# One-hot records stored with the two halves of different gathers, and a target loop of six gathers on a ring of six

## The reference, cut to what matters

```python
ef = concatenate([nf[src], nf[dst], traj[:, None]], axis=-1)
msg = leaky_relu(ef @ We.T + be, negative_slope=0.01)
red = segment_sum(msg, dst, num_segments=nf.shape[0])
h = leaky_relu(concatenate([nf, red], axis=-1) @ Wn.T + bn, negative_slope=0.01)
```

## Time and profile before

| | us |
|---|---|
| median of 3 runs | 10442.16 |
| lowest and highest | 10429.43, 10443.02 |
| profiled execution, first to last instruction (span) | 10466.8 |
| span less the median of the runs | 24.6 |
| first target phase, gathers L1695, first to last start | 3310.8 to 4534.3 |
| layers' target phases together, gathers L1832, first to last start | 5273.9 to 10353.2 |

### The profile page before, as it was taken

How to read it: one execution, slowest core, us unless ns; L and a number is a source line. 1 busy time by engine, 2 the same in 40 slices (tenths; PEclk the granted TensorE clock), 3 DMA queues, 4 the chain that set the end, 5 groups by cost and what they waited for, 6 DMA issues and landing times. The chain is left out here.

```text
span 10466.8 us, 546251 instructions
## 1 busy us (share of the span) xinstructions
PE 8877.0 (85%) x200294; PEld 7617.9 (73%) x200294; DVE 8717.3 (83%) x16671; ACT 7435.1 (71%) x19555; POOL 4345.7 (42%) x4286
## 2 busy tenths in 40 slices
PE   7999999546997666659988888999888989989987
PEld 6999999324775555558877777787777768877775
DVE  6999999456998999978878787787887878778877
ACT  7888887003666999966777777677777767677776
POOL 0000000455002777734455555345555534455553
PEclk9999999656999999969999999999999999999998
DMA  1000000023666888849988888698788859978875
GB/s 44 8 10 8 8 8 6 19 42 101 210 209 203 253 253 254 248 115 290 294 256 248 248 249 215 208 293 273 248 248 248 243 160 293 295 247 249 249 247 150
DMA packets 1298246, 1948.78 MB, mean 186 GB/s; under 512 B 192607, under 2 KB 831081, under 8 KB 1297257
## 3 DMA queue, kind: packets, MB, share of 16 engines
q1 hardware_dynamic: 1052054, 1285.20, 36.7%
q0 software_dynamic: 245248, 650.66, 24.2%
q10 hardware_dynamic: 304, 4.93, 0.1%
HBM read 1225.54 MB, written 719.25 MB: 186 GB/s over the span
## 5 line engine op out<-in xcount | busy, mean ns | idle before, releaser
L1832 POOL DMA_INDIRECT work<-rows,oct_at x1752 | 2148.6, 1226 | 1609.9 <-DVE work L1957 1448.1
L1663 PEld LDWEIGHTS bank<-work 128*128 128x128 fp8e4 (+1 forms) x56064 | 1938.1, 98 | 477.3 <-issue 289.5
L1663 PE MATMUL bank<-work 128*128 128x64 bf16 x56064 | 2107.4, 193 | 110.8 <-issue 87.7
L1957 DVE TENSOR_TENSOR work<-bank,work 128x512 f32<-128x512 f32 x1752 | 1206.8, 689 | 768.1 <-PE bank L1908 616.1
L1908 PE MATMUL bank<-work 128*128 128x64 bf16 x42048 | 1600.5, 193 | 186.8 <-issue 138.5
L1607 PE MATMUL bank<-work 128*128 128x64 bf16 x34560 | 1567.4, 193 | 5.7 <-issue 5.7
L1908 PEld LDWEIGHTS bank<-work 128*128 128x128 fp8e4 x42048 | 1391.5, 98 | 214.4 <-issue 171.8
L1607 PEld LDWEIGHTS bank<-work 128*128 128x128 fp8e4 x34560 | 1412.4, 98 | 174.5 <-issue 9.7
L1858 ACT CAST work<-bank 128x512 bf16<-128x512 f32 x1752 | 1026.4, 586 | 542.6 <-issue 374.2
L1626 DVE TENSOR_SCALAR work<-bank,part 128x512 fp8e4<-128x512 f32 x1440 | 1029.0, 750 | 283.0 <-PE bank L1587 282.6
L1961 DVE SCALAR_TENSOR_TENSOR bank<-work 128x512 f32<-128x512 f32 x1752 | 1216.9, 695 | 4.5
(11 more groups left out here) (363 smaller groups left out, 20361.0 us busy)
## 6 DMA issues: line engine op xcount, KB each, us to landing
work<-hits_g SPq DMA_DIRECT2D x1752, 256.0 KB
rows<-work SPq DMA_DIRECT2D x1440, 256.0 KB
hits_g<-work SPq DMA_DIRECT2D x584, 256.0 KB
rows<-work SPq DMA_DIRECT2D x480, 260.0 KB
work<-hits_s SPq DMA_DIRECT2D x720, 128.0 KB, 3.1
work<-rows,oct_at POOLq DMA_INDIRECT x2336
hits_s<-work SPq DMA_DIRECT2D x240, 128.0 KB
side<-meta POOLq DMA_DIRECT2D x720, 20.0 KB, 3.1
```

Source lines behind the costliest of these rows:

```text
L1663: last = ten.matmul(to[:, 0:D], hits_of(j), piece_of(j), start=j == 0 and k == 0, stop=j == OCT - 1 and k == 2, skip_group_check=True)
L1832: pool.indirect_dma_start(octs[g % ROWS], None, table_octs, bass.IndirectOffsetOnAxis(ap=oct_at[:, g:g + 1], axis=0)).then_inc(s_octs[g % ...
L1957: vec.tensor_tensor(total[g % 2], z[g % BANKS][:, :], octs[g % ROWS], ALU.add).then_inc(s_added, 1)
```

## The change

Record r now holds the turned half of gather r and the edge half of gather r-5. PE uses exactly these two in one step (the sum lags by five steps), so a record is used in one step only. The DRAM tensor has 5 more records. In the first target phase each gather's buffer is stored by two DMAs of 128 KB, in rows of 1 KB: the turned half into record g, the edge half into record g+5; the buffer is free when both have landed (32 instead of 16).

In the layers the ring is of 6 records. The load of record r waits for the sum of gather r-11, which is in step r-6. The first five records are loaded as turned halves alone, five more at the end as edge halves alone; records 6 to 10 also wait for the first multiplication with the record 6 before. The loop body is 6 gathers: 12 straight, 94 bodies (93 jumps back), 8 straight. ACT loads three window numbers in every third step. WINDOWS and LOWS become 6, so that they go into the body of 6.

The diff, cut to the lines that change and a few around them:

```diff
@@ -44,7 +44,8 @@
 GROUP_LOT = 2
-AROUND = 12
+AROUND = 6
+SCATTER = 5
@@ -108,7 +109,7 @@
     hits_s = dram("hits_s", [NS // GROUP_LOT, P, GROUP_LOT * SLOTS // 2], BF16)
-    hits_g = dram("hits_g", [NG, P, OCT * P], BF16)
+    hits_g = dram("hits_g", [NG + SCATTER, P, OCT * P], BF16)
     rows0 = dram("rows0", [NS * P, QUAD * (D + 1)], F32)
@@ -1240,11 +1241,11 @@
-    def laps(engine, count, step, size=LAP):
-        for q in range(size):
-            step(q, q, 0)
-        with engine.Fori(1, count // size - 1) as i:
+    def laps(engine, count, step, size=LAP, first=1):
+        for g in range(first * size):
+            step(g, g % size, g // size)
+        with engine.Fori(first, count // size - 1) as i:
             for q in range(size):
@@ -1664,6 +1665,14 @@
+    def turned_half(ap):
+        return ap[:, 0:OCT * P // 2]
+    def edge_half(ap):
+        return ap[:, OCT * P // 2:OCT * P]
@@ -1699,7 +1708,11 @@
                 syn.wait_ge(s_cast, g + 1)
-                syn.dma_start(hits_g[bass.ds(g, 1), :, :].rearrange("g p c -> (g p) c"), hits_home[q % 4]).then_inc(s_out[q % 4], 16)
+                settle(syn, "sync", g)
+                syn.dma_start(turned_half(hits_g[bass.ds(g, 1), :, :].rearrange("g p c -> (g p) c")),
+                              turned_half(hits_home[q % 4])).then_inc(s_out[q % 4], 16)
+                syn.dma_start(edge_half(hits_g[bass.ds(g + SCATTER, 1), :, :].rearrange("g p c -> (g p) c")),
+                              edge_half(hits_home[q % 4])).then_inc(s_out[q % 4], 16)
@@ -1707,7 +1720,7 @@
                 sca.wait_ge(s_hits, g + 1)
-                at_least(sca, s_out[q % 4], 16 * (2 * lap + q // 4))
+                at_least(sca, s_out[q % 4], 32 * (2 * lap + q // 4))
                 settle(sca, "scalar", g)
@@ -1785,13 +1798,13 @@
             for n in range(4):
-                e.wait_ge(s_out[n], 16 * NG // 4)
-        return [(s_out[n], 16 * NG // 4) for n in range(4)]
+                e.wait_ge(s_out[n], 32 * NG // 4)
+        return [(s_out[n], 32 * NG // 4) for n in range(4)]
...
         s_octs = [sem_of(f"sums_octs{n}", True) for n in range(GATHERED)]
-        HITS, ROWS, WINDOWS, BANKS, MIDS, LOWS = 12, 4, 4, 6, 6, 4
+        HITS, ROWS, WINDOWS, BANKS, MIDS, LOWS = 6, 4, 6, 6, 6, 6
         s_in = [sem_of(f"sums_in{n}", True) for n in range(HITS)]
@@ -1800,7 +1813,7 @@
         since, since_octs = past * NG, number * (NG // GATHERED) * 16
-        since_in = [past * 16 * len(range(n, NG, HITS)) for n in range(HITS)]
+        since_in = [past * 16 * len(range(n, NG + SCATTER, HITS)) for n in range(HITS)]
         room = Room(work, WORK)
@@ -1810,7 +1823,7 @@
         z, sums = bank[0:BANKS], bank[BANKS:8]
-        LESS, LESSER, LOW, SCATTER, KEEP = 2, 3, 4, 5, 6
+        LESS, LESSER, LOW, KEEP, NUMBERS = 2, 3, 4, 6, 3
         by_vector = lambda g: g % 2 > 0
@@ -1834,18 +1847,27 @@
         def _(syn):
-            def load(g, q):
-                if isinstance(g, int) and g >= NG:
-                    return
-                at_least(syn, s_sum, g - HITS + 1, since)
-                syn.dma_start(hits_home[q % HITS], hits_g[bass.ds(g, 1), :, :].rearrange("g p c -> (g p) c")).then_inc(s_in[q % HITS], 16)
+            def load(r, q):
+                part_of = lambda ap: ap
+                if isinstance(r, int):
+                    if r < SCATTER:
+                        part_of = turned_half
+                    if r >= NG:
+                        part_of = edge_half
+                    if HITS <= r < HITS + SCATTER:
+                        syn.wait_ge(s_before, since + r - HITS + 1)
+                at_least(syn, s_sum, r - HITS - SCATTER + 1, since)
+                settle(syn, "sync", r)
+                syn.dma_start(part_of(hits_home[q % HITS]),
+                              part_of(hits_g[bass.ds(r, 1), :, :].rearrange("g p c -> (g p) c"))).then_inc(s_in[q % HITS], 16)
...
                 load(g, g)
-            laps(syn, NG, step, AROUND)
+            laps(syn, NG, step, AROUND, 2)
@@ -1871,11 +1893,12 @@
                 at_least(sca, s_before, g - WINDOWS + 1, since)
-                sca.copy(window[q % WINDOWS].unsqueeze(1), tabs[:, 1, bass.ds(next_windows[q % 4], 1), :]).then_inc(s_window, 1)
+                sca.copy(window[q % WINDOWS].unsqueeze(1), tabs[:, 1, bass.ds(next_windows[q % NUMBERS], 1), :]).then_inc(s_window, 1)
             def step(g, q, lap):
-                if q % 4 == 0:
-                    next_windows[:] = registers(sca, win_g[0:1, bass.ds(g, 4)], NW - 1)
+                if q % NUMBERS == 0:
+                    count = min(NUMBERS, NG - g) if isinstance(g, int) else NUMBERS
+                    next_windows[:] = registers(sca, win_g[0:1, bass.ds(g, count)], NW - 1)
                 window_of(g, q)
@@ -1884,7 +1907,7 @@
-            laps(sca, NG, step, AROUND)
+            laps(sca, NG, step, AROUND, 2)
             for g in range(NG, NG + LESSER + 3):
@@ -1922,11 +1945,11 @@
-            def scatter(g, q, low_made):
+            def scatter(g, q, low_made, record):
                 ten.wait_ge(s_low[by_vector(q)], low_made)
...
                 settle(ten, "tensor", g)
-                hits = hits_home[q % HITS].bitcast(FP8)[:, OCT * P:2 * OCT * P].rearrange("p (j c i) -> p j c i", c=P, i=2)
+                hits = record.bitcast(FP8)[:, OCT * P:2 * OCT * P].rearrange("p (j c i) -> p j c i", c=P, i=2)
                 each = lambda ap: lambda j: ap[:, j * D:(j + 1) * D]
@@ -1938,11 +1961,12 @@
                 if begun(g, SCATTER):
-                    scatter(g - SCATTER, (q - SCATTER) % AROUND, lows_made(lap, q - SCATTER))
-            laps(ten, NG, step, AROUND)
+                    scatter(g - SCATTER, (q - SCATTER) % AROUND, lows_made(lap, q - SCATTER), hits_home[q % HITS])
+            laps(ten, NG, step, AROUND, 2)
             for g in range(NG, NG + SCATTER):
-                scatter(g - SCATTER, (g - SCATTER) % AROUND, lows_made(0, g - SCATTER))
+                ten.wait_ge(s_in[g % HITS], since_in[g % HITS] + 16 * (g // HITS + 1))
+                scatter(g - SCATTER, (g - SCATTER) % AROUND, lows_made(0, g - SCATTER), hits_home[g % HITS])
                 if g - LESS < NG:
```

## The result

Both kernels ran on one chip: before 10442.59 us (median of 4 runs), after **10531.44 us** (median of 4, 10526.74 to 10534.60). The ratio is 1.0085, 95% interval 1.0071 to 1.0099: 89 us slower. The forecast was 10426 with a range of 10385 to 10485, and no change as the likeliest. It was wrong: the time lies above the range, and what happened is rival C, at more than its upper price.

The account below looks back on a forecast made before the run. DVE was taken to bound the first target phase, with the store ring close behind, and a chain over PE, DVE and ACT the layers. Terms -7+5-14 = -16 gave 10426 us, range 10385 to 10485.

Parts of the forecast that it names:

- rival C: First target phase: the ring of store buffers takes over from DVE, +58 for the store, 10479 us in all; chance 0.07.
- Part 3: First target phase: two stores instead of one, 584 times, free the buffer later; +5 us, bounds 0 to 58.
- The delay: First target phase: with two stores the buffer is free 0.3 us later, bounds 0 and 0.66 us.
- The price of a delay: First target phase: delay beyond the 0.26 us slack costs a quarter of itself a step, 584 steps; at most 58 us.
- The hidden slack: First target phase: one turn of the store ring needs 8.07 us where four steps take 8.33, slack 0.26 us.
- Part 4: Layers' loops: bodies of 6 gathers, 144 more jumps at -0.10 us each, -14 us; loads of window numbers 0.
- rival A: Layers' loops: the short body runs faster, 144 x -0.23 = -33 us, 10402 us in all; chance 0.35.
- rival B: Layers' loops: jumps delay ACT's window copy, 0.30 us x 144 = +43 us, 10483 us in all; chance 0.13.
- Part 2: Start of each layer: fewer record loads ahead of the first gathers, 2.3 us saved a layer, -7 us.
- Parts 1 and 5: Layers: the ring of 6 skewed records instead of 12, and the straight ends behind the loop; 0 us each.
- E: Layers: a record comes late as the lead is shorter, 88 us, 10514 us in all; chance 0.03.
- D: Layers' loops: each extra jump fetches code at 5.65 us, +814 us, 11240 us in all; chance 0.02.

Follow-up runs that it names:

- E7: Changed kernel with the layers' loop body of 12 and load of four window numbers of before: 10532.19 us, ratio 1.0079 to the kernel before.
- E1: Kernel before with each record stored as two DMAs of 128 KB, nothing else: 9833.49 us, ratio 1.0082 to the kernel before, on a faster chip.
- E11: Kernel before with ACT loading three window numbers instead of four, on a faster chip: 9850.95 us, ratio 1.0103 to the kernel before.
- E3: Changed kernel with both halves stored by one DMA of 256 rows of 1 KB: 9900.91 us, ratio 1.0147 to the kernel before, faster chip.
- C1: The changed kernel again, unedited, against the kernel before: 10538.65 us, ratio 1.0084.
- E8: Changed kernel with six store buffers, body of 12 and load of four window numbers: 9754.09 us, ratio 1.0003 to the kernel before, faster chip.
- E2: Changed kernel with the edge half stored as soon as it is cast: 9883.43 us, ratio 1.0135 to the kernel before; first target phase 1239.2 us.
- E4: Changed kernel with six store buffers instead of four: 9877.60 us, ratio 1.0124 to the kernel before; first target phase 1240.3 us.
- E5: Kernel before with ACT loading three window numbers instead of four, on a chip like the first: 10458.96 us, ratio 1.0006 to the kernel before.
- E10: Kernel before with six store buffers in the first target phase, on a faster chip: 9753.88 us, ratio 1.0001 to the kernel before.

## Why the prediction was wrong

**Part 3, the two stores, failed.** It forecast +5 us between 0 and +58; the runs show +80 (E7 against before, on the first kind of chip) and +80 (E1). In three steps:

- *The delay.* This is the step that failed. I took 0.3 us, "nearer the 128 KB row", where a load of 128 KB landed in 3.1 us. The cast came 3.99 us after the second half's issue, nearly as late as with the whole record of 256 KB before. That row is a load of the source phase, not a store in this mix. The upper bound, 0.55+0.11, was nearly right on this chip: the shown turn is 8.67-8.07 = 0.60 us longer. On the faster chip the delay was 0.76 us (E1 against E11).
- *The price of a delay.* (0.60-0.26)/4 x 584 is 50 us for the turn shown, and the phase grew by 66.9 us, 0.115 a step (0.131 between 3700 and 4300). By DVE's time a step grew by 0.09 us of idle, (800-766.24)/361 for (800-797.55)/384, and by 0.046 us of busy time, 766.24/361 for 797.55/384; that DVE is busy longer once it pauses was in no term. Nor had I a term for this: of two rings that are close to each other, the step follows not the longer one on average but the later one each time, and DVE's own bound is still near, since it waits for ACT 84 times only. This last is argued, not shown. So +58 was no upper bound.
- *The hidden slack.* 0.26 us came from one turn of one timeline. Another sign was at hand: 54 waits for the store and 150 more for "issue" at the same cast before. DVE's own waits before were only 13.0 us for ACT, but those stops told how close the ring was.

Rival C had the mechanism, the place and the sign, "DVE under 98%" as its mark, and 0.07 as its chance, on the strength of that one row of another phase. Its own argument, that half a microsecond of second issue is more than the slack, was right, and E3 puts some 63 of 89 us on that issue.

**Part 4, the loop bodies.** -14 us forecast, +6.5 by the medians and +14.5 by the traces measured for jumps and loads together (C1 less E7), small and near the noise, within the bounds for the jumps of -0.23 to +0.51 each. The gain that I read from the half-laps isn't there (rival A), nor are the +43 of rival B. The load of window numbers, costed at 0 because "no load without a jump left a gap", failed. That held for loads of four numbers, 0.31 us; the changed kernel loads three, 0.70 us, and 580 gaps came where 279 were forecast. The duration of the old load was in the trace, that of the new one was not, and I should have given it bounds. The Trainium skill ("Runtime: NRT & Kernel Launch", Instruction fetch mechanics, in its note on TENSOR_LOAD) puts a load of registers from HBM at about 200 ns a register even for bulk. Here the numbers come from SBUF; the steps between one, two and three of them on ACT (278, 494, 704 ns, 0.21 us apart) are near that figure, and four (309 ns) don't fit it.

**Part 2, the starts.** -7 us forecast. The first add came 2.0 us sooner after SP's first load (forecast 2.3) and the waits for rows are gone, as said. But E7, where the loop in the layers is that of before, has layers of 3753.6 us in all against 3755.2: the saving did not reach the end, or only 1.6 us of it. The add waits 53 us more for PE in its place.

**Parts 1 and 5** held: PE waited for records 6 times (before 10), and E7 and E8 show no price of the ring of six. So **E** is excluded. **D** is too: between 5500 and 6200 us the changed kernel has 23 packets of q14, as before, with some 28 more jumps on each of the three engines (an estimate from the step), and a layer grew by 2 to 4 us, not by 271. The rule of the Trainium skill that D quotes ("Runtime: NRT & Kernel Launch", Instruction fetch mechanics) is one on taken branches; that a loop's end stalls by it was a step of my own.

The engine time that I forecast from the source phase's rows, 12.8 us a record, came out 12.0 to 12.3, and it did not bind.

Of the marks, stores are 2 x 584, but ACT's waits counted as `hits_g` were 36.4 us and so under my 60 although the ring was the bound. They stood under "issue". The gathers of 1000 us were 471, below 473 to 476. The first add came 5.04 us after SP's first load, where "within 5" was the mark.

## What to carry to other kernels

When one DMA becomes two and its buffer is free only when both have landed, count the ring anew: here it was the last issue plus a full landing of its own, not the bytes halved. A ring whose turn is within 5% of the bound (8.07 against 8.33 us here) has to be priced as the bound, and a split that is needed anyway can be paid with two more buffers or an earlier first half: E2 and E4 each bring the phase back. A register load with another count is a new operation; look for its duration or bound it. And an edit whose cost hides on one chip (E5, ratio 1.0006) can cost 1% on another of the same kind (E11, 1.0103).

## What the runs showed of the hardware

- A store of 128 KB took as long as one of 256 KB in this mix: 3.99 and 4.03 us from issue to the next use in the turns shown, 3.67 us (E1) and 3.48 (E11) from issue to landing on the mean. A second issue on SP came 0.50 us after the first on the mean (changed kernel; 0.57 in E1).
- Rows of 1 KB cost 12.0 to 12.3 us of DMA engine time for 256 KB, rows of 2 KB 10.9 to 11.0, and a DMA of 256 KB in them landed 0.60 us later (E3 against E11).
- Loading 1, 2, 3 or 4 numbers into ACT's registers took 278, 494, 704 and 309 ns at the median. Only the four-number load is out of line; why was not looked into.
- The same program took 10443 and 10452 us in two sets of runs and 9753 and 9754 on two other chips, at the same mean granted clock or nearly (0.949 for the kernel before, 0.957 for E10 and E11). The first target phase is about as long on both kinds without the split store (1236.9 and 1233.0) and longer on the faster with it (1326.3 in E1, 1308.0 in the changed kernel). The time ahead of it is 177 us shorter on the faster kind (E11 against E5), the layers' target phases are 14% shorter (E8 against E7), and PE's unexplained stops before its first matmul of a step are 71 us instead of 314 in the same kernel (E11 against E5). What makes them differ stays open.
